# Group-norm statistics averaged on TensorE as a rounded value and its rest, two columns in one single-pass product

## The chip, the core and the metric

The kernel runs on one core of a Trainium2 chip. What counts is device time in microseconds (us) of one execution. The core has five engines with a queue each: TensorE (PE in the profile, with its weight loads listed as PEld), VectorE (DVE), ScalarE (ACT), GpSimd (POOL) and SyncE (SP, which here only starts transfers). Engines wait for one another through semaphores; each runs its own queue in order.

## What is computed

The input is 8 sequences of 512 tokens with 128 features. After a layer norm, four layers of the block below run one after the other, and a mixture of 8 experts is added to the result.

```python
def block(h, p):
    r = _retention(h, wk)                      # masked linear attention
    m = r @ w1 + b1
    a, gate = jnp.split(m, 2, axis=-1)
    m = a * jax.nn.silu(gate) @ w2 + b2
    m = _groupnorm1(m, gg, gb)                 # mean and variance over all tokens AND features
    y = m + h
    f = jax.nn.gelu(y @ wf1 + bf1_, approximate=False) @ wf2 + bf2_
    return (_layernorm(f + y, lg, lb), None)
```

`_groupnorm1` takes one mean and one variance over the 512 x 128 values of a sequence. This document is about how these two numbers are put together.

## The kernel before, in words

Features lie on the 128 partitions, tokens along the free axis, so that the activations of a sequence are one tile of 128 x 512. An item is one sequence in one layer; there are 32, numbered 0 to 31 (item n is sequence n % 8 of layer n // 8). The program of each engine is a loop over slots, `for n in range(ITEMS + ...): slot(n)`, and in each slot every stage handles an item of its own, so that some ten items are in work at once. The order of the stages within a slot is written out by hand for each engine, and the engine follows it in order: an instruction whose semaphore isn't there holds up all that stand behind it.

The eight PSUM banks are shared by stages that take turns. `vacated(n, (reader, back), ...)` makes TensorE wait until the reader of the former contents is through. Bank 4 goes round between projection (`G_BANK`), scores (`SCORE_BANK`), the group-norm averages (`GN_BANK`) and the second half of the feed-forward product (`FEED_B_BANK`).

The group norm of an item goes to and fro between TensorE and VectorE:

- `group_stats`, `group_aggr` (VectorE): mean and variance of each partition, from PSUM. `group_means` adds the bias `B2` to the mean: `gn_m`.
- `group_mean` (TensorE, L388): a product of `mean_of` (128 x 128, all 1/128) with the column `gn_m`; every partition receives the mean over the partitions.
- `group_dev` (VectorE, L897, L898): the deviation `gn_d` of the own mean from it, and `gn_b2`. `group_parts` (L902): `gn_p`, deviation squared plus own variance.
- `group_var` (TensorE, L392): the same kind of product with `gn_p`.
- `group_veps` (VectorE, L907): variance plus epsilon, `gn_v`. It is the last reader of bank 4, and signals `gn_veps`.
- GpSimd's `pow`, then `group_scale`, `group_coef` (VectorE) and `group_norm` (ScalarE).

On VectorE, work for other items stands between these steps: behind `group_means` `set_y` (L929), behind `group_dev` the offsets of another item's layer norm (L956, L959), and between `group_parts` and `group_veps` the steps `gate` (L873), `add_experts` (L981) and `set_z` (L936). On TensorE, `feed_a` (L406) and `feed_b` (L399) stand right behind `group_var`. `feed_b` writes bank 4, so it has this line:

```python
vacated(n, (gn_veps, -1), (gelu_b, 1))
```

that is, it waits for `group_veps` of the item whose averages stand in the bank. The next one behind it, `gram` (L315), waits for `prod_b` of VectorE's `weigh_b` (L967).

A product of float32 operands appears in the trace as two pairs of weight load and multiplication; one of float32r operands (a float32 rounded to what a single pass takes; `xn`, `ot`, `b_w` and `expert_w` are such) as one pair. `product` (L246, L247, L250) makes three single-pass products of rounded values and their rests in place of a float32 one.

Of the kernel before, what the change touches and what calls it, by code (L numbers as in the profile page):

```python
# [5 lines left out]
F32 = mybir.dt.float32  # L6
F32R = mybir.dt.float32r
ALU = mybir.AluOpType
# [3 lines left out]
P = 128  # L12
EPS = 1e-5
# [3 lines left out]
HALF_B1A, HALF_B1G, B1G, B2, GN_G, GN_B, BF1A, BF1B, BF2, LN_G, LN_B = range(11)  # L17
# [8 lines left out]
def retention_moe(nc, x, Wkqv, Wm1, bm1, Wm2, bm2, gn_g, gn_b, Wf1, bf1, Wf2, bf2, ln_g, ln_b,  # L26
# [15 lines left out]
    with ctx:  # L42
        def sb(name, *shape, dtype=F32):
            return ctx.enter_context(nc.sbuf_tensor(name, list(shape), dtype))

        def sem(name):
            return ctx.enter_context(nc.semaphore(name))

        def several(names):
            return [sem(name) for name in names.split()]  # L50
# [6 lines left out]
        mean_of = sb("mean_of", P, P)  # L57
        minus_half = sb("minus_half", P, C)
# [9 lines left out]
        params = sb("params", P, 11, L)  # L68
# [31 lines left out]
        gn_mv = sb("gn_mv", P, 2, 2)  # L100
        gn_m, gn_d, gn_b2, gn_p, gn_v, gn_r, gn_s, gn_c = (
# [35 lines left out]
        GN_BANK = banks[4]  # L137
# [12 lines left out]
        ones_set, means_set, zeros_set, stored = several("ones_set means_set zeros_set stored")  # L150
# [21 lines left out]
        gn_stats, gn_aggr, gn_means, gn_mean, gn_dev, gn_parts, gn_var, gn_veps, gn_rstd, gn_scale, gn_coef, gn_done = several(  # L172
            "gn_stats gn_aggr gn_means gn_mean gn_dev gn_parts gn_var gn_veps gn_rstd gn_scale gn_coef gn_done")
# [55 lines left out]
        def _(pe):  # L229
# [153 lines left out]
            def group_mean(n):  # L383
                if n == 0:
                    pe.wait_ge(means_set, 1)
                pe.wait_ge(gn_means, n + 1)
                vacated(n, (scores_set, -3), (gelu_b, 2))
                pe.matmul(GN_BANK[:, 0:1], mean_of[:, :], gn_m[:, n % 2:n % 2 + 1], start=True, stop=True).then_inc(gn_mean, 1)  # L388

            def group_var(n):  # L390
                pe.wait_ge(gn_parts, n + 1)
                pe.matmul(GN_BANK[:, 2:3], mean_of[:, :], gn_p[:, n % 2:n % 2 + 1], start=True, stop=True).then_inc(gn_var, 1)  # L392
# [333 lines left out]
        def _(dve):  # L726
            def cols(t, n, width=1):
                return t[:, n % 2:n % 2 + 1]
# [160 lines left out]
            def group_means(n):  # L889
                l = n // NB  # L890
                dve.wait_ge(gn_aggr, n + 1)
                dve.tensor_tensor(cols(gn_m, n), gn_mv[:, n % 2, 0:1], params[:, B2, l:l + 1], ALU.add).then_inc(gn_means, 1)

            def group_dev(n):
                l = n // NB
                dve.wait_ge(gn_mean, n + 1)
                dve.tensor_scalar(cols(gn_d, n), GN_BANK[:, 0:1], -1.0, cols(gn_m, n), ALU.mult, ALU.add).then_inc(gn_dev, 1)  # L897
                dve.tensor_scalar(cols(gn_b2, n), GN_BANK[:, 0:1], -1.0, params[:, B2, l:l + 1], ALU.mult, ALU.add)  # L898

            def group_parts(n):  # L900
                dve.wait_ge(gn_dev, n + 1)
                dve.scalar_tensor_tensor(cols(gn_p, n), cols(gn_d, n), cols(gn_d, n), gn_mv[:, n % 2, 1:2],  # L902
                                         ALU.mult, ALU.add).then_inc(gn_parts, 1)

            def group_veps(n):
                dve.wait_ge(gn_var, n + 1)
                dve.tensor_scalar(cols(gn_v, n), GN_BANK[:, 2:3], EPS, None, ALU.add).then_inc(gn_veps, 1)  # L907
# [98 lines left out]
            dve.memset(mean_of[:, :], 1.0 / P).then_inc(means_set, 1)  # L1006
            read_in(0)
# [252 lines left out]
```

## Time and profile before

| | us |
|---|---|
| median of 3 runs | 462.77 (462.64 to 463.01) |
| the profiled execution | 463.61 |
| its span in the profile | 461.7 |
| TensorE busy, share of the span | 440.6, 95% |
| VectorE busy | 385.1, 83% |
| ScalarE busy | 220.0, 48% |
| GpSimd busy | 162.2, 35% |

The span runs from the first to the last instruction; the execution's own time is 1.9 us longer. TensorE's granted clock was 0.992 of full speed over the execution. A busy share says how long an engine had something in it, not that its work set the time; that is read from the chain that ended last, the work that is followed back from the last instruction, at each step to what released it.

### The profile page before, as it was taken

What the parts mean: (1) busy time and instruction counts of PE and PEld (TensorE: products, weight loads), DVE (VectorE), ACT (ScalarE), POOL (GpSimd) and SP (SyncE); (2) the same over time, 40 slices, a digit from 0 to 9 for tenths busy, and PEclk for the clock granted to TensorE, in tenths of its full rate; (3) what the DMA queues carried; (4) which work ended last, traced back from release to release, by engine and by line L of the source; (5) the groups of instructions that cost most, each with busy time, mean ns of one, the idle gap of its engine ahead of it and who ended that gap; (6) DMA issues with size and microseconds to landing.
All of it is one profiled execution on the core that took longest, in us unless ns stands there. A gap on an engine that the chain in (4) does not pass through costs nothing.

```text
span 461.7 us, 7880 instructions
## 1 busy us (share of the span) xinstructions
PE 440.6 (95%) x2302; PEld 318.2 (69%) x2302; DVE 385.1 (83%) x1347; ACT 220.0 (48%) x411; POOL 162.2 (35%) x198
## 2 busy tenths in 40 slices
PE   3999999999999999999999999999999999999982
PEld 2888767777777777777777777777777777765440
DVE  5699989899888877987878877787788887999996
ACT  2125464555554544555555445455555544545331
POOL 3233203634343333542222332433223332334542
PEclk9999999999999999999999999999999999999996
DMA  8900000000000000000000000000000000000113
GB/s 234 253 1 1 1 1 0 2 0 1 1 1 2 1 1 0 2 0 1 1 1 0 2 0 1 1 2 2 1 1 1 1 0 2 1 1 12 34 31 107
DMA packets 13497, 8.20 MB, mean 18 GB/s; under 512 B 608, under 2 KB 13456, under 8 KB 13456
## 3 DMA queue, kind: packets, MB, share of 16 engines
q1 hardware_dynamic: 13376, 7.68, 5.9%
q8 instruction: 20, 0.33, 0.3%
q14 instruction: 21, 0.17, 0.1%
q10 hardware_dynamic: 80, 0.02, 0.0%
HBM read 5.60 MB, written 2.10 MB: 17 GB/s over the span
## 4 chain that ended last, share of the span: by engine, by line
PE 87%; DVE 8%; issue 2%; ACT 1%; DMA 1%; DVEq 0%; POOL 0%; POOLq 0%
PE pair L406 6%; PE bank L325 6%; PE pair L331 6%; PE bank L308 6%; PE bank L381 6%; PE bank L399 6%; PE bank L417 5%; PE bank L254 5%; PE bank L413 5%; PE bank L315 5%; PE bank L250 5%; PE pair L333 4%; PE bank L246 4%; PE bank L247 4%; PE bank L357 3%
## 5 line engine op out<-in xcount | busy, mean ns | idle before, releaser
L1126 POOL TENSOR_TENSOR gn_r<-gn_v,minus_half 128x1 f32<-128x1 f32 x32 | 17.5, 548 | 174.1 <-DVE gn_v L907 174.1
L1136 POOL TENSOR_TENSOR sum_four<-prod 128x512 f32<-128x512 f32 x32 | 40.5, 1265 | 74.6 <-DVE prod L967 74.6
L615 ACT ACTIVATE a_in<-bank,params 128x512 f32<-128x512 f32 x32 | 22.0, 688 | 84.7 <-PE bank L250 84.7
L647 ACT ACTIVATE va<-bank,ln_off,ln_r 128x128 f32<-128x128 f32 x128 | 48.3, 465 | 17.8 <-DVE ln_off L959 17.8
L331 PEld LDWEIGHTS pair<-va,scores 128*128 128x128 f32 x256 | 43.0, 190 | 18.9 <-issue 16.3
L967 DVE TENSOR_TENSOR prod<-bank,route 128x512 f32<-128x512 f32 x64 | 43.7, 683 | 8.6 <-PE bank L250 8.5
L331 PE MATMUL pair<-va,scores 128*128 128x129 f32 x256 | 49.3, 275 | 1.1 <-issue 1.1
L246 PE MATMUL bank<-expert_w,xn 128*128 128x512 f32 x64 | 42.3, 661 | 1.5 <-DVE zt L936 1.5
L325 PEld LDWEIGHTS bank<-gt,vt 128*128 128x128 f32 x256 | 33.5, 191 | 14.5 <-issue 13.1
L1131 POOL TENSOR_TENSOR ln_r<-ln_v,minus_half 128x4 f32<-128x4 f32 x32 | 32.7, 1023 | 14.3 <-DVE ln_v L951 13.5
L333 PE MATMUL pair<-past,gt 128*128 128x129 f32 x192 | 37.1, 275 | 0.0
L315 PEld LDWEIGHTS bank<-va 128*128 128x128 f32 x192 | 27.2, 199 | 14.1 <-issue 14.1
L604 ACT COPY gt<-bank 128x512 f32<-128x512 f32 x32 | 18.7, 585 | 37.0 <-PE bank L308 37.0
L942 DVE BATCH_NORM_STATS2 ln_st<-bank 128x6 f32<-128x128 f32 x128 | 28.4, 283 | 8.8 <-PE bank L254 8.8
L406 PE MATMUL pair<-y,wf 128*128 128x512 f32 x64 | 35.3, 633 | 0.0
L325 PE MATMUL bank<-gt,vt 128*128 128x128 f32 x256 | 33.8, 275 | 0.3 <-ACT gt L604 0.3
L621 ACT ACTIVATE tanh_g<-pair,params 128x512 f32<-128x512 f32 x32 | 22.0, 687 | 25.3 <-PE pair L250 25.3
L381 PE MATMUL bank<-mixed,wm 128*128 128x512 f32 x64 | 33.1, 598 | 0.4 <-ACT gn_out L628 0.4
L308 PE MATMUL bank<-vt,a_w 128*128 128x512 f32 x64 | 33.3, 603 | 0.0
L417 PE MATMUL bank<-gelu,wf 128*128 128x512 f32 x64 | 32.9, 596 | 0.0
L413 PE MATMUL bank<-gelu,wf 128*128 128x512 f32 x64 | 32.9, 595 | 0.0
L399 PE MATMUL bank<-y,wf 128*128 128x512 f32 x64 | 32.8, 594 | 0.0
(159 smaller groups left out, 1097.7 us busy)
## 6 DMA issues: line engine op xcount, KB each, us to landing
x_in<-in_L_attn_x_dram SPq DMA_DIRECT2D x8, 256.0 KB, 5.4
out_dram<-x_in SPq DMA_DIRECT2D x8, 256.0 KB, 2.3
wf<-in_L_attn_Wf_dram SPq DMA_DIRECT2D x2, 512.0 KB, 6.6
kqv<-in_L_attn_Wkqv_dram SPq DMA_DIRECT2D x1, 576.0 KB, 6.2
expert_rows<-in_L_ffn_We_dram SPq DMA_DIRECT2D x1, 512.0 KB, 8.2
wm<-in_L_attn_Wm_dram SPq DMA_DIRECT2D x1, 384.0 KB, 7.2
wm<-in_L_attn_Wm_dram SPq DMA_DIRECT2D x1, 256.0 KB, 5.0
expert_b<-in_L_ffn_be_dram SPq DMA_DIRECT2D x16, 4.0 KB
```

What stands on the lines that cost most here:

```text
L246: pe.matmul(dst, weights(0), moving(0), start=True, stop=False)
L308: pe.matmul(G_BANK[:, :], a_w[:, l, :], vt[:, k, :], start=True, stop=True).then_inc(g_done, 1)
L315: mm = pe.matmul(GRAM_BANK[:, c * AUG:c * AUG + D + 1], va[:, k, c, 0:D], va[:, k, c, 0:D + 1], start=True, stop=True)
L325: mm = pe.matmul(SCORE_BANK[:, of], vt[:, k, of], gt[:, n % 2, of], start=True, stop=True)
L331: mm = pe.matmul(dst, scores[:, n % 2, of], va[:, n % NB, c, 0:D + 1], start=True, stop=(c == 0))
L333: mm = pe.matmul(dst, gt[:, n % 2, of], past[:, n % 3, c - 1, 0:D + 1], start=False, stop=True)
L381: pe.matmul(MIXED_BANK[:, :], wm2[:, n // NB, :], mixed[:, :], start=True, stop=True).then_inc(mixed_done, 1)
L399: pe.matmul(FEED_B_BANK[:, :], wf1[:, n // NB, D:], y[:, n % 2, :], start=True, stop=True).then_inc(f1b_done, 1)
L406: pe.matmul(FEED_A_BANK[:, :], wf1[:, n // NB, 0:D], y[:, n % 2, :], start=True, stop=True).then_inc(f1a_done, 1)
L413: pe.matmul(BACK_BANK[:, :], wf2[:, n // NB, 1, :], gelu[:, n % 2, 1, :], start=True, stop=False)
L417: pe.matmul(BACK_BANK[:, :], wf2[:, n // NB, 0, :], gelu[:, n % 2, 0, :], start=False, stop=True).then_inc(f2_done, 1)
L647: last = act.activation(va[:, n % NB, c, 0:D], Z_BANK[:, c * P:(c + 1) * P], ACT.Identity, bias=ln_off[:, i, c:c + 1], scale=ln_r[:, i, c: ...
```

## The change

Both averages are made as single-pass products in float32r. VectorE writes each of the two inputs as two columns: the value rounded to float32r, and what the rounding left over. One product of the matrix `mean_r` (a float32r copy of `mean_of`) with the two columns gives the averages of both, and the reader adds or subtracts both PSUM columns, as two per-partition scalar operands.

```diff
+        mean_r = sb("mean_r", P, P, dtype=F32R)
+        gn_m2, gn_p2 = (sb(name, P, 2, 2, dtype=F32R) for name in ("gn_m2", "gn_p2"))
...
             def group_mean(n):
                 if n == 0:
-                    pe.wait_ge(means_set, 1)
-                pe.wait_ge(gn_means, n + 1)
+                    pe.wait_ge(mean_r_set, 1)
+                pe.wait_ge(gn_m_rest, n + 1)
                 vacated(n, (scores_set, -3), (gelu_b, 2))
-                pe.matmul(GN_BANK[:, 0:1], mean_of[:, :], gn_m[:, n % 2:n % 2 + 1], start=True, stop=True).then_inc(gn_mean, 1)
+                pe.matmul(GN_BANK[:, 0:2], mean_r[:, :], gn_m2[:, n % 2, :], start=True, stop=True).then_inc(gn_mean, 1)
 
             def group_var(n):
-                pe.wait_ge(gn_parts, n + 1)
-                pe.matmul(GN_BANK[:, 2:3], mean_of[:, :], gn_p[:, n % 2:n % 2 + 1], start=True, stop=True).then_inc(gn_var, 1)
+                pe.wait_ge(gn_p_rest, n + 1)
+                pe.matmul(GN_BANK[:, 2:4], mean_r[:, :], gn_p2[:, n % 2, :], start=True, stop=True).then_inc(gn_var, 1)
...
             def group_means(n):
                 l = n // NB
                 dve.wait_ge(gn_aggr, n + 1)
+                dve.tensor_tensor(gn_m2[:, n % 2, 0:1], gn_mv[:, n % 2, 0:1], params[:, B2, l:l + 1], ALU.add).then_inc(gn_m_rounded, 1)
                 dve.tensor_tensor(cols(gn_m, n), gn_mv[:, n % 2, 0:1], params[:, B2, l:l + 1], ALU.add).then_inc(gn_means, 1)
+                dve.wait_ge(gn_m_rounded, n + 1)
+                dve.wait_ge(gn_means, n + 1)
+                dve.tensor_scalar(gn_m2[:, n % 2, 1:2], gn_m2[:, n % 2, 0:1].bitcast(F32), -1.0, cols(gn_m, n),
+                                  ALU.mult, ALU.add).then_inc(gn_m_rest, 1)
 
             def group_dev(n):
                 l = n // NB
                 dve.wait_ge(gn_mean, n + 1)
-                dve.tensor_scalar(cols(gn_d, n), GN_BANK[:, 0:1], -1.0, cols(gn_m, n), ALU.mult, ALU.add).then_inc(gn_dev, 1)
-                dve.tensor_scalar(cols(gn_b2, n), GN_BANK[:, 0:1], -1.0, params[:, B2, l:l + 1], ALU.mult, ALU.add)
+                dve.tensor_scalar(cols(gn_d, n), cols(gn_m, n), GN_BANK[:, 0:1], GN_BANK[:, 1:2],
+                                  ALU.subtract, ALU.subtract).then_inc(gn_dev, 1)
+                dve.tensor_scalar(cols(gn_b2, n), params[:, B2, l:l + 1], GN_BANK[:, 0:1], GN_BANK[:, 1:2],
+                                  ALU.subtract, ALU.subtract)
 
             def group_parts(n):
                 dve.wait_ge(gn_dev, n + 1)
-                dve.scalar_tensor_tensor(cols(gn_p, n), cols(gn_d, n), cols(gn_d, n), gn_mv[:, n % 2, 1:2],
-                                         ALU.mult, ALU.add).then_inc(gn_parts, 1)
+                dve.tensor_scalar(gn_p2[:, n % 2, 0:1], cols(gn_d, n), cols(gn_d, n), gn_mv[:, n % 2, 1:2],
+                                  ALU.mult, ALU.add).then_inc(gn_p_rounded, 1)
+                dve.tensor_scalar(cols(gn_p, n), cols(gn_d, n), cols(gn_d, n), gn_mv[:, n % 2, 1:2],
+                                  ALU.mult, ALU.add).then_inc(gn_parts, 1)
+                dve.wait_ge(gn_p_rounded, n + 1)
+                dve.wait_ge(gn_parts, n + 1)
+                dve.tensor_scalar(gn_p2[:, n % 2, 1:2], gn_p2[:, n % 2, 0:1].bitcast(F32), -1.0, cols(gn_p, n),
+                                  ALU.mult, ALU.add).then_inc(gn_p_rest, 1)
 
             def group_veps(n):
                 dve.wait_ge(gn_var, n + 1)
-                dve.tensor_scalar(cols(gn_v, n), GN_BANK[:, 2:3], EPS, None, ALU.add).then_inc(gn_veps, 1)
+                dve.tensor_scalar(cols(gn_v, n), GN_BANK[:, 2:3], GN_BANK[:, 3:4], EPS, ALU.add, ALU.add).then_inc(gn_veps, 1)
...
             dve.memset(mean_of[:, :], 1.0 / P).then_inc(means_set, 1)
+            dve.wait_ge(means_set, 1)
+            dve.tensor_copy(mean_r[:, :], mean_of[:, :]).then_inc(mean_r_set, 1)
             read_in(0)
             normalise_in(0)
```

On VectorE four instructions come in for each item. This is its queue around the group norm of one middle item before, from `group_means` (L892) to `group_veps` (L907); a row has line, operation, output, inputs, shape and the semaphores that it waits for:

```order
L892 TENSOR_TENSOR gn_m<-gn_mv,params 128x1 [waits gn_aggr]
L929 SCALAR_TENSOR_TENSOR y<-vt,g_prev,gn_out 128x512 [waits f1b_done,f1a_done,gn_done]
L897 TENSOR_SCALAR gn_d<-bank,gn_m 128x1 [waits gn_mean]
L898 TENSOR_SCALAR gn_b<-bank,params 128x1
L956 TENSOR_TENSOR ln_mr<-ln_mv,ln_r 128x4 [waits ln_rstd]
L959 TENSOR_SCALAR ln_off<-ln_mr 128x4 [waits v_set,ln_mr_set]
L902 SCALAR_TENSOR_TENSOR gn_p<-gn_d,gn_mv 128x1 [waits gn_dev]
L873 SCALAR_TENSOR_TENSOR gated<-pair,params,a_in 128x512 [waits tanh_set,a_in_set]
L981 TENSOR_TENSOR x_in<-x_in,sum_one 128x128 [waits x_shifted,one_set]
L936 SCALAR_TENSOR_TENSOR zt<-bank,params,y 128x512 [waits z_turned,f2_done]
L907 TENSOR_SCALAR gn_v<-bank 128x1 [waits gn_var]
```

And the same place after, as far as `gate`. The names `gn_m` and `gn_p` here stand for both the old tiles and the new `gn_m2` and `gn_p2`:

```order
L894 TENSOR_TENSOR gn_m<-gn_mv,params 128x1 [waits gn_aggr]
L895 TENSOR_TENSOR gn_m<-gn_mv,params 128x1
L898 TENSOR_SCALAR gn_m<-gn_m 128x1 [waits gn_means,gn_m_rounded]
L944 SCALAR_TENSOR_TENSOR y<-vt,g_prev,gn_out 128x512 [waits f1b_done,f1a_done,gn_done]
L904 TENSOR_SCALAR gn_d<-gn_m,bank 128x1 [waits gn_mean]
L906 TENSOR_SCALAR gn_b<-params,bank 128x1
L971 TENSOR_TENSOR ln_mr<-ln_mv,ln_r 128x4 [waits ln_rstd]
L974 TENSOR_SCALAR ln_off<-ln_mr 128x4 [waits v_set,ln_mr_set]
L911 TENSOR_SCALAR gn_p<-gn_d,gn_mv 128x1 [waits gn_dev]
L913 TENSOR_SCALAR gn_p<-gn_d,gn_mv 128x1
L917 TENSOR_SCALAR gn_p<-gn_p 128x1 [waits gn_parts,gn_p_rounded]
L875 SCALAR_TENSOR_TENSOR gated<-pair,params,a_in 128x512 [waits tanh_set,a_in_set]
```

`group_means` has become three instructions (L894, L895, L898) in place of one, the third of which waits for the other two; `group_parts` likewise (L911, L913, L917 in place of L902). Nothing else has moved: `group_veps` (now L922) still stands behind `gate`, `add_experts` and `set_z`.

On TensorE the order of the products is untouched. This is its queue around `group_var` of one middle item before, with `feed_a` and `feed_b` behind it:

```order
L250 MATMUL bank<-expert_w,xn 128x512
L392 MATMUL bank<-gn_p,mean_of 128x1 [waits gn_parts]
L406 MATMUL pair<-y,wf 128x512 [waits o_set,y_set]
L399 MATMUL bank<-y,wf 128x512 [waits gn_veps,y_set]
L315 MATMUL bank<-va 128x129 [waits prod_b,v_set]
```

And after, where line numbers are two higher:

```order
L252 MATMUL bank<-expert_w,xn 128x512
L394 MATMUL bank<-gn_p,mean_r 128x2 [waits gn_p_rest]
L408 MATMUL pair<-y,wf 128x512 [waits o_set,y_set]
L401 MATMUL bank<-y,wf 128x512 [waits gn_veps,y_set]
L317 MATMUL bank<-va 128x129 [waits prod_b,v_set]
```

The product has two columns where it had one, and waits for `gn_p_rest` where it waited for `gn_parts`. `feed_b` still waits for `gn_veps`, and `gram` for `prod_b`.

## Rows read from the trace of the kernel before

**Rows 1.** the page: busy time by engine, and the chain that ended last, by engine
```profile
PE 440.6 (95%) x2302; PEld 318.2 (69%) x2302; DVE 385.1 (83%) x1347; ACT 220.0 (48%) x411; POOL 162.2 (35%) x198
...
PE 87%; DVE 8%; issue 2%; ACT 1%; DMA 1%; DVEq 0%; POOL 0%; POOLq 0%
```

**Rows 2.** chain that ended last: start us, us of the chain, engine, output, line, instructions
```profile
202.99 0.88 PE bank L254 x8
...
210.07 0.11 PE bank L388 x2
210.19 0.50 PE bank L357 x4
...
212.23 0.12 PE bank L392 x2
212.35 0.97 PE pair L406 x2
213.31 0.86 PE bank L399 x2
```

**Rows 3.** timeline of VectorE in the same period: start us, duration us, operation, idle before
```profile
208.69 0.15 DVE L892 TENSOR_TENSOR gn_m<-gn_mv,params 128x1 f32<-128x1 f32 x1
208.75 0.74 DVE L929 SCALAR_TENSOR_TENSOR y<-vt,g_prev,gn_out 128x512 f32<-128x512 f32 x1
210.23 0.22 DVE L897 TENSOR_SCALAR gn_d<-bank,gn_m 128x1 f32<-128x1 f32 x1 [0.73 <-PE bank L388]
...
210.49 0.15 DVE L956 TENSOR_TENSOR ln_mr<-ln_mv,ln_r 128x4 f32<-128x4 f32 x1
210.67 0.17 DVE L959 TENSOR_SCALAR ln_off<-ln_mr 128x4 f32<-128x4 f32 x1
210.75 0.21 DVE L902 SCALAR_TENSOR_TENSOR gn_p<-gn_d,gn_mv 128x1 f32<-128x1 f32 x1
210.90 0.75 DVE L873 SCALAR_TENSOR_TENSOR gated<-pair,params,a_in 128x512 f32<-128x512 f32 x1
...
212.43 0.15 DVE L907 TENSOR_SCALAR gn_v<-bank 128x1 f32<-128x1 f32 x1
```

**Rows 4.** timeline of TensorE in the same period: multiplications, and the weight load (PEld)
```profile
209.91 0.28 PE L388 MATMUL bank<-gn_m,mean_of 128*128 128x1 f32 x2
...
212.72 0.19 PEld L399 LDWEIGHTS bank<-y,wf 128*128 128x128 f32 x1 [0.24 <-issue]
...
213.15 0.59 PE L399 MATMUL bank<-y,wf 128*128 128x512 f32 x1
```

**Rows 5.** timeline of TensorE and VectorE, the same places for item 27
```profile
389.21 0.28 PE L388 MATMUL bank<-gn_m,mean_of 128*128 128x1 f32 x2
...
389.53 0.22 DVE L897 TENSOR_SCALAR gn_d<-bank,gn_m 128x1 f32<-128x1 f32 x1 [0.71 <-PE bank L388]
...
392.10 0.15 DVE L907 TENSOR_SCALAR gn_v<-bank 128x1 f32<-128x1 f32 x1
...
392.36 0.30 PEld L399 LDWEIGHTS bank<-y,wf 128*128 128x128 f32 x2 [0.57 <-issue]
392.45 1.04 PE L399 MATMUL bank<-y,wf 128*128 128x512 f32 x2
```

**Rows 6.** single lines over the whole run: durations ns min/median/max
```profile
L746 DVE TENSOR_SCALAR va<-x_in,in_mv,in_r x32: 332/340/1425, 6.4 to 49.9; 128x128 f32<-128x128 f32 x32
...
L951 DVE TENSOR_SCALAR ln_v<-ln_mv x32: 169/170/922, 77.5 to 450.8; 128x4 f32<-128x4 f32 x32
...
L388 PE MATMUL bank<-gn_m,mean_of x64: 164/250/271, 45.4 to 430.7; 128*128 128x1 f32 x64
```

**Rows 7.** waits over the whole run: us in total, times, longest
```profile
DVE gn_d L897 <- PE bank L388: 17.9, 27, 0.7
```

**Rows 8.** timeline of GpSimd in the period of rows 2
```profile
212.65 0.55 POOL L1126 TENSOR_TENSOR gn_r<-gn_v,minus_half 128x1 f32<-128x1 f32 x1 [4.77 <-DVE gn_v L907]
```

**Rows 9.** one stretch: its length, busy us (instructions) of PE, PEld, DVE, ACT, POOL; clock
```profile
422.00:432.00 10.00, 9.17 (x29) 4.43 (x29) 9.83 (x34) 4.17 (x8) 4.44 (x5) 1.00 0.09 26
```

More of the change, by code:

```diff
@@ L149, in retention_moe @@
         x_loaded = [sem(f"x_loaded{k}") for k in range(NB)]
-        ones_set, means_set, zeros_set, stored = several("ones_set means_set zeros_set stored")
+        ones_set, means_set, mean_r_set, zeros_set, stored = several("ones_set means_set mean_r_set zeros_set stored")
         shift_done, kqv_shifted, kqv_turned, kqv_t_set, folded, a_set, b_rounded, b_set = several(
@@ L171, in retention_moe @@
             "ot_set ot_rest a_in_set tanh_set gated_set mixed_set")
-        gn_stats, gn_aggr, gn_means, gn_mean, gn_dev, gn_parts, gn_var, gn_veps, gn_rstd, gn_scale, gn_coef, gn_done = several(
-            "gn_stats gn_aggr gn_means gn_mean gn_dev gn_parts gn_var gn_veps gn_rstd gn_scale gn_coef gn_done")
+        gn_stats, gn_aggr, gn_m_rounded, gn_means, gn_m_rest, gn_mean, gn_dev, gn_p_rounded, gn_parts, gn_p_rest, gn_var, gn_veps, gn_rstd, gn_scale, gn_coef, gn_done = several(
+            "gn_stats gn_aggr gn_m_rounded gn_means gn_m_rest gn_mean gn_dev gn_p_rounded gn_parts gn_p_rest gn_var gn_veps gn_rstd gn_scale gn_coef gn_done")
         y_set, f1a_done, f1b_done, gelu_a, gelu_b, f2_done, z_set, z_turned = several(
```

## The prediction

> **What bounds the kernel now.** First read the page: TensorE is busy for 95% of the span, and the chain that ended last is 87% TensorE and 8% VectorE [rows 1]. Shorter work on TensorE should shorten the run, if nothing makes TensorE wait in its place. Then the chain itself in one period of the middle, about item 13: TensorE goes from product to product without a gap [rows 2]. VectorE is the follower: between `group_means` and `group_dev` it stands still for 0.73 us until the product of L388 is through [rows 3], and in 27 of the 32 items it waits there [rows 7]. After that, from L897 to L907, it has no idle time at all [rows 3]. That is the stretch to look at, since TensorE's `feed_b` (L399) can't start before `group_veps` (L907) has emptied bank 4.
>
> How much room does that wait have? L907 ends at 212.43 + 0.15 = 212.58. The first weight load of L399 is at 212.72, the multiplication at 213.15 [rows 3, 4]. In item 27, where the VectorE stretch happened to be longer, L907 ends at 392.25 and the load is at 392.36: 0.11 us is the least that the signal takes here. The multiplication follows the load by 0.09 only [rows 5]; I count 0.11, since that is what a load costs where nothing hides it (below). So the room is (0.14 - 0.11) + (0.43 - 0.11) = 0.35 us. Item 27 bears it out: from L897 to the end of L907 it takes 392.25 - 389.53 = 2.72 us, where item 13 takes 212.58 - 210.23 = 2.35, and yet L399 starts 3.24 us after L388 in both (392.45 - 389.21, 213.15 - 209.91) [rows 3, 4, 5]. A delay of 0.37 was just absorbed; little more will be.
>
> **What the change gives TensorE.** A float32 product is two loads and two multiplications. With 1 column to move, the second load lies bare, and so does the first load of the next product. In the chain L388 has 0.11, and the four transposes of L357 behind it take 0.50, where eight elsewhere take 0.88, so 0.06 more than four should: 0.17 in all. L392 has 0.12, and L406 behind it 0.97 where its twin L399 has 0.86: 0.23 in all [rows 2]. The single-pass product keeps one load, which lies under the 512 columns ahead of it as the first one does now. The neighbour's bare load (0.06 and 0.11) stays, with some 0.02 for the short product. Saved: 0.09 + 0.11, so 0.20 us for an item. It can't be over 0.40, the whole of both. The Trainium skill (VectorE: DVE Perf Modes, the section on the TRN2 errata) has a matmul of few columns at 60 cycles, 25 ns at 2.4 GHz: by that the two multiplications that go would give only 0.05. The rows show the bare load as the larger part, and the measurement decides. As L399 turns out below, the sum is the same with either.
>
> **What it costs VectorE**, from start to start. An instruction with no per-partition scalar occupies the queue for 0.06 to 0.07 (L892 to L929), one with one for 0.13 (L897 to L956: two in 0.26). One that needs its predecessor's result starts 0.03 after that has ended (L956 ends at 210.64, L959 starts at 210.67) [rows 3]. Two scalars are seen in L746 alone: 0.34 long, with 128 elements, where L951 without scalars and with 4 elements has 0.17 [rows 6]. If those elements account for about 0.07, each scalar adds 0.05; so I take 0.27 for the duration and 0.185 for the step. Bounds: as with one scalar (0.21 and 0.13), and L746's own 0.34, with a step of 0.26.
>
> - `group_means`: the second `gn_m` starts 0.07 later, the rest waits for its end (0.15 + 0.03), and `set_y` follows 0.13 on: 0.38 in place of 0.07, so +0.31. It is covered by the 0.73 of idle time ahead of `group_dev`. TensorE's product L388 starts at 209.91 [rows 4]; its input is there at 208.84 now and would be at 209.16 after. Without that cover it would cost the 0.31.
> - `group_dev`: two instructions with two scalars, +0.11 (0 to 0.26).
> - `group_parts`: 0.185 to the second, 0.27 + 0.03 until the rest may start, 0.13 to `gate`: 0.62 in place of 0.15, so +0.47 (0.35 to 0.61).
> - `group_veps`: one scalar, ends 0.07 later.
> - `mean_r`: one copy of 128 elements at the start, while VectorE waits for the first input: nothing, at worst L746's 0.34, once.
>
> From L897 to the end of L907 that is +0.65 (0.42 to 0.94). Against it, L897 starts earlier, as one multiplication ends 0.17 after its start where two end after 0.28 [rows 4, 6]: -0.10. Net +0.55 where there is room for 0.35. So L399 starts 3.24 + 0.20 = 3.44 us after L388. Without the wait it would be 3.24 - 0.20 = 3.04, since both savings lie ahead of it. **TensorE then stands still for 0.40 us ahead of `feed_b`**, gives back all it gained, and the period grows by 0.20. Queued behind L399 are `gram` and the next round of everything, so it isn't made up. `prod_b` for `gram` comes late by about as much as L399 itself, and adds nothing. Of the other results that come later on VectorE here (`mixed`, z, the rest of `ot`), the first use stands behind L399 and `gram` in TensorE's queue.
>
> **The sum.** Items 3 to 26 look like item 13: 24 x 0.20 = +4.8 (with the bounds 24 x -0.03 to 24 x +0.49; the upper would need every unknown at its dearest, so I stop halfway at 0.33, +7.9). Item 27 has its room used up by the 0.37 already: +0.5; 28 as the others, +0.2. From item 29 on VectorE has no idle time to hide anything in (9.83 of 10 us [rows 9]), so the full +0.96 of an item (0.31 + 0.11 + 0.47 + 0.07) counts, partly overlapped with TensorE's own work: three items, +2.5. Tail: +3.2 (1.5 to 4.5). Items 0 to 2, where fewer stages run and TensorE waits for this loop: an estimate of +1.0 (0 to 1.5), from up to 0.4 for each plus the late `gate`. Together +9.0. The profiled execution (463.61, 1.9 over its span) would become 472.6; the median of 462.77 stood 0.8 below it, which gives **471.8 us**.
>
> **The rivals.**
>
> - *The late `group_veps`*, as above: 471.8. Chance 0.72.
> - *Two scalars cost no more than one.* Growth 0.42 - 0.10 = 0.32, just under the room of 0.35: L399 starts 0.03 earlier, and only the ends pay. 24 x -0.03 + 1.5 + 0.3 = +1.1, so 463.9. For it: only L746 speaks of two scalars, and its element part is my guess. Chance 0.14, half of it within 0.2%.
> - *TensorE keeps its gain, faster.* One mechanism: `group_veps` comes in time because the new instructions are cheap; from the point where the net growth is under 0.35 there is some gain, and under 0.15 the full one (0.35 less the 0.20 by which TensorE comes early). 27 x -0.20 + 1.0 at the end = -4.4, so 458.4. For it: the 87% of the chain, and a step of 0.07 for plain instructions. Against it: `group_parts` alone has two dependent durations in series, 0.35 at the least by these rows. Chance 0.10.
> - *GpSimd holds up the new instructions.* L951 has a median of 0.17 and a maximum of 0.92 [rows 6], so something stretches small instructions at times. Were it 0.6 more in each of 8 items, that is +4.8, so 476.6. Against it: GpSimd stood idle for 4.77 us up to 212.65 [rows 8], which covers all four new ones. Chance 0.04. The Trainium skill (SBUF — State Buffer, the section on who interferes with whom) makes that lock one between VectorE with two SBUF inputs and GpSimd, for a whole instruction; what rows 8 show leaves it no opportunity in the middle of the run.
>
> Range: the first case from its low side to nearly its high one, and the second: 463.5 to 476. Narrower for the likeliest alone: 467 to 476. About 0.2% (0.9 us) is what a measurement can tell from no change. Faster by more: 0.11 (the third, and a bit of the second). Within: 0.08. Slower: 0.81.
>
> **What would show it.** In the profile after: L399 (now L401) with idle time on TensorE ahead of it of about 0.4 us in each middle period, and its first load 0.11 behind the end of L907 (now L922); L388 as a single multiplication, and the transposes behind it still at 0.50; from the start of `group_dev` to the end of `group_veps` 3.0 us in place of 2.35; `group_parts` spread over 0.62; period 0.20 longer. The prediction is wrong if two-scalar instructions are short, so that this stretch stays under 2.7 us, or if the load of L399 can slip further than 0.32 without its product being late.

## The result, and the profile after

The changed kernel is **slower: 476.98 us** (median of 5 runs, 476.59 to 477.05) against 462.85 (5 runs, 462.64 to 463.59); ratio 1.0281, interval 1.0247 to 1.0315. That is +14.1 us where +9.0 was forecast, and 0.98 us beyond the range's upper end of 476. The profiled execution took 476.70 (span 474.9, which is 13.2 more than the 461.7 of before). Ratios, here and below, are the recorded ones with their 95% intervals, and can differ a little from the quotient of two medians. Some executions in the later sessions, of the kernel before too, had a lower granted clock (down to 0.975) and took up to 6 us longer, so medians below carry 1 to 2 us of scatter and the periods are the sharper measure.

The page of the kernel after, busy time by engine and the chain by engine [for before: rows 1]:
```profile
PE 442.3 (93%) x2238; PEld 308.1 (65%) x2238; DVE 413.3 (87%) x1476; ACT 221.4 (47%) x411; POOL 162.2 (34%) x198
...
PE 60%; DVE 28%; issue 10%; DMA 1%; DVEq 1%; ACT 0%; POOL 0%; POOLq 0%
```
64 multiplications and 64 loads are gone, and 129 VectorE instructions have come, with 28 us of busy time. TensorE's busy time has not shrunk: part of a wait is booked as busy there, as shown below. The plainest sign is the chain of work that ended last. TensorE's share fell from 87% to 60%, and VectorE's rose from 8% to 28%.

A period is the time from one item's mean product to the next one's. One period of that chain, about item 13 (start us, us of the chain, engine, output, line) [rows 2]:
```profile
214.79 0.05 PE bank L390
214.84 0.03 issue
214.87 0.04 DVE gn_d L904
...
217.07 0.74 DVE zt L951
217.81 0.14 DVE gn_v L922
217.95 0.14 issue
218.09 1.10 PE bank L401 x2
219.18 0.67 PE bank L317 x6
...
227.83 0.05 PE bank L390
```
Before, the chain never left TensorE in this stretch. Now it goes out to VectorE at L390 and comes back at L401 (`feed_b`, L399 before). From the mean product to the end of `feed_b` it takes 219.18 - 214.79 = 4.39 us, where it took 213.31 + 0.86 - 210.07 = 4.10: +0.29, and this period is 227.83 - 214.79 = 13.04.

VectorE in the same period (start us, duration us, operation, idle time before it) [rows 3]:
```profile
214.87 0.28 DVE L904 TENSOR_SCALAR gn_d<-gn_m,bank 128x1 f32<-128x1 f32 x1 [0.24 <-PE bank L390]
215.07 0.27 DVE L906 TENSOR_SCALAR gn_b<-params,bank 128x1 f32<-128x1 f32 x1
...
215.52 0.27 DVE L911 TENSOR_SCALAR gn_p<-gn_d,gn_mv 128x1 fp32r<-128x1 f32 x1
215.71 0.26 DVE L913 TENSOR_SCALAR gn_p<-gn_d,gn_mv 128x1 f32<-128x1 f32 x1
216.08 0.21 DVE L917 TENSOR_SCALAR gn_p<-gn_p 128x1 fp32r<-128x1 f32 x1
216.21 0.74 DVE L875 SCALAR_TENSOR_TENSOR gated<-pair,params,a_in 128x512 f32<-128x512 f32 x1
...
217.07 0.74 DVE L951 SCALAR_TENSOR_TENSOR zt<-bank,params,y 128x512 f32<-128x512 f32 x1
217.73 0.21 DVE L922 TENSOR_SCALAR gn_v<-bank 128x1 f32<-128x1 f32 x1
```
The idle time ahead of `group_dev` shrank from 0.73 to 0.24, since `group_means` takes more and the shorter product is through earlier (`group_dev` starts 0.24 after it, and 0.32 before); from there to the end of `group_veps` VectorE needs 217.94 - 214.87 = 3.07 us where it needed 2.35. Look at L917: L913 has ended at 215.97, and L917 starts only at 216.08, 0.11 later.

TensorE and its weight loads (PEld) in the same period, GpSimd's row, and the mean product of items 3 and 27 [rows 4, 5, 8]:
```profile
83.59 0.17 PE L390 MATMUL bank<-gn_m,mean_r 128*128 128x2 f32 x1
...
214.63 0.17 PE L390 MATMUL bank<-gn_m,mean_r 128*128 128x2 f32 x1
...
216.68 0.17 PE L394 MATMUL bank<-gn_p,mean_r 128*128 128x2 f32 x1
216.71 1.10 PE L408 MATMUL pair<-y,wf 128*128 128x512 f32 x2
218.02 0.55 POOL L1143 TENSOR_TENSOR gn_r<-gn_v,minus_half 128x1 f32<-128x1 f32 x1 [5.39 <-DVE gn_v L922]
218.06 0.30 PEld L401 LDWEIGHTS bank<-y,wf 128*128 128x128 f32 x2 [1.07 <-issue]
218.09 1.10 PE L401 MATMUL bank<-y,wf 128*128 128x512 f32 x2 [0.27 <-DVE gn_v L922]
...
398.48 0.17 PE L390 MATMUL bank<-gn_m,mean_r 128*128 128x2 f32 x1
```
L401's load is at 218.06, 0.12 behind the end of `group_veps` at 217.94. The multiplication is recorded 0.03 after its load, yet it has 1.10 us in the chain, against 0.86 in [rows 2]: these 0.24 are the rest of the wait, booked as work. That is why the page's busy time for TensorE went up.

The waits over the whole run, total us, times and longest [rows 7]:
```profile
DVE gn_d L904 <- PE bank L390: 5.5, 22, 0.3
```
And the view of single lines over the whole run: durations of L390 and L917, ns min/median/max [rows 6], and under L922 who waited for it, us and times:
```profile
L390 PE MATMUL bank<-gn_m,mean_r x32: 164/165/272, 45.3 to 443.2; 128*128 128x2 f32 x32
...
L917 DVE TENSOR_SCALAR gn_p<-gn_p x32: 212/214/217, 46.6 to 445.5; 128x1 fp32r<-128x1 f32 x32
...
L922 DVE TENSOR_SCALAR gn_v<-bank x32: 209/211/217, 47.7 to 446.5; 128x1 f32<-128x1 f32 x32
...
  PE bank L401: 9.0, 28
```
L390 is one multiplication of 165 ns where L388 was two. In 28 of 32 items TensorE has recorded idle time ahead of `feed_b`. Between 90 and 350 us the kernel before has no wait of TensorE for VectorE at all.

A stretch near the end: its length, busy us of PE, PEld, DVE, ACT and POOL, then the granted clock [rows 9]:
```profile
435.00:445.00 10.00, 8.28 (x24) 3.72 (x24) 9.72 (x32) 2.99 (x6) 4.42 (x5) 1.00 0.09 28
```
VectorE is busy for 9.72 of 10 us and TensorE for 8.28, and the chain runs through VectorE there, as before. The granted clock is 1.00 in this stretch, falls to 0.50, the lower of its two levels, only for the last 7.5 us of the span (7.6 before), and is 0.992 over the whole of either execution; it has no part in the loss.

Where the 13.2 us of the span lie, by the start of the mean product in items 3 and 27 (the periods of the middle are 13.04 to 13.14 long, 13.07 in the mean, but for items 10, 17 and 19; those of before are 12.76, but for items 3 and 19):

| stretch | before | after | difference | forecast |
|---|---|---|---|---|
| up to item 3 | 82.05 | 83.59 | +1.5 | +1.0 |
| item 3 to 27, 24 periods | 307.16 | 314.89 | +7.7 | +4.8 |
| item 27 to the end of the span | 72.5 | 76.4 | +3.9 | +3.2 |

### The profile page after: what moved, and what is told of

The parts are those of the page before. It is cut to its first block, busy times and chain, and to the rows that moved or that the text cites. A ratio compares the mean times of both kernels' runs of the same rounds, so it can differ in the third digit from the quotient of the medians.

```text
span 474.9 us, 7945 instructions
## 1 busy us (share of the span) xinstructions
PE 442.3 (93%) x2238; PEld 308.1 (65%) x2238; DVE 413.3 (87%) x1476; ACT 221.4 (47%) x411; POOL 162.2 (34%) x198
## 4 chain that ended last, share of the span: by engine, by line
PE 60%; DVE 28%; issue 10%; DMA 1%; DVEq 1%; ACT 0%; POOL 0%; POOLq 0%
PE bank L401 6%; PE pair L333 6%; PE bank L310 5%; PE bank L327 5%; PE bank L256 5%; PE bank L383 5%; PE bank L317 5%; DVE zt L951 4%; PE bank L415 4%; PE pair L335 4%; PE bank L248 3%; PE bank L252 2%; PE bank L249 2%; DVE prod L982 2%; DVE gn_b L906 2%
## 5 line engine op out<-in xcount | busy, mean ns | idle before, releaser
L401 PE MATMUL bank<-y,wf 128*128 128x512 f32 x64 | 34.9, 627 | 9.1 <-DVE gn_v L922 9.0
L317 PEld LDWEIGHTS bank<-va 128*128 128x128 f32 x192 | 27.1, 199 | 14.2 <-issue 14.2
```

What stands on the lines that cost most here:

```text
L317: mm = pe.matmul(GRAM_BANK[:, c * AUG:c * AUG + D + 1], va[:, k, c, 0:D], va[:, k, c, 0:D + 1], start=True, stop=True)
L401: pe.matmul(FEED_B_BANK[:, :], wf1[:, n // NB, D:], y[:, n % 2, :], start=True, stop=True).then_inc(f1b_done, 1)
```

## The experiments

**Theory A**, as in the prediction: `feed_b` is gated by the path `group_dev` to `group_veps` on VectorE, with room for 0.35 us. While this path grows by less, TensorE keeps at least a part of its gain; over it, the gain and the excess are lost. **Rivals**: the costs simply add (each new instruction costs its time, whatever TensorE does), and VectorE as a whole has become too full, at 87%.

### One half of the change at a time

The mean alone in the new form (`group_var`, `group_parts` and `group_veps` as before):
```diff
-pe.matmul(GN_BANK[:, 2:4], mean_r[:, :], gn_p2[:, n % 2, :], start=True, stop=True).then_inc(gn_var, 1)
+pe.matmul(GN_BANK[:, 2:3], mean_of[:, :], gn_p[:, n % 2:n % 2 + 1], start=True, stop=True).then_inc(gn_var, 1)
...
```


> Only the mean is averaged the new way; the variance keeps its float32 product, its one instruction and its one column. Theory A: from the start of group_dev to the end of group_veps only the two subtractions grow (+0.13), against 0.08 of earlier start: within the room of 0.35. So L388's half of TensorE's gain stays (0.11 x 24 = 2.6), and the ends lose about 2 for the 0.44 more on VectorE: 462.2. Theory B: 0.44 of 1.12 us of new VectorE work, so 40% of the 14.1 lost: 468.5.

Measured: 463.78 us (10 runs), ratio 0.999 (0.9953 to 1.0027), span 460.1, period 12.65. TensorE doesn't wait between items 3 and 27, and the period is 0.11 shorter than the 12.76 of before. The extra instructions of `group_means` and `group_dev` are paid outside the middle: the 24 periods give 2.5 back, and from item 27 on 1.2 are lost again. The way from item 0 to item 3 takes 0.5 more too (37.19 against 36.67), though item 0 starts 0.8 earlier in this execution and hides it.

The variance alone (`group_mean`, `group_means` and `group_dev` as before):
```diff
-pe.matmul(GN_BANK[:, 0:2], mean_r[:, :], gn_m2[:, n % 2, :], start=True, stop=True).then_inc(gn_mean, 1)
+pe.matmul(GN_BANK[:, 0:1], mean_of[:, :], gn_m[:, n % 2:n % 2 + 1], start=True, stop=True).then_inc(gn_mean, 1)
...
```


> Only the variance is averaged the new way; the mean keeps its float32 product and its old instructions. Theory A: the path grows by 0.54 in group_parts and 0.07 in group_veps, 0.61 against 0.35 of room: TensorE waits ahead of L401, and the period is 12.76 + 0.26 = 13.02, 24 x 0.26 + 3 at the ends: 472. The gain on L392 is lost whole. Theory B: 60% of 14.1: 471.3. It is the middle period and the idle time ahead of L401 that tell, not the total.

Measured: 473.53 us (4 runs), ratio 1.0193 (1.013 to 1.0257), period 13.00 to 13.03, 13.01 in the mean. The load of `feed_b` comes 0.12 behind the end of `group_veps` in every item of the middle. The halves are -0.11 and +0.25 for a period, but both together are +0.30: behind the wait that the variance half opens, the mean half no longer gives its 0.11, and costs 0.05, by its longer `group_dev`. The wait itself comes from `group_parts`, with 0.06 more from the longer `group_veps`.

### The new VectorE work with the old products

```diff
-pe.matmul(GN_BANK[:, 0:2], mean_r[:, :], gn_m2[:, n % 2, :], start=True, stop=True).then_inc(gn_mean, 1)
+pe.matmul(GN_BANK[:, 0:1], mean_of[:, :], gn_m[:, n % 2:n % 2 + 1], start=True, stop=True).then_inc(gn_mean, 1)
...
-pe.matmul(GN_BANK[:, 2:4], mean_r[:, :], gn_p2[:, n % 2, :], start=True, stop=True).then_inc(gn_var, 1)
+pe.matmul(GN_BANK[:, 2:3], mean_of[:, :], gn_p[:, n % 2:n % 2 + 1], start=True, stop=True).then_inc(gn_var, 1)
```
`group_dev` and `group_veps` are those of before; the rounded parts and rests are made, but TensorE multiplies the float32 values.

> The new VectorE instructions of group_means and group_parts are all there, and TensorE waits for the rests, but both averages are the float32 products of before, and group_dev and group_veps read one column as before; the rounded columns are computed and not used. So it has VectorE's cost without TensorE's gain. Theory A: TensorE's gain never counted in the middle, since it lies ahead of the wait in L401. L401 comes at 0.32 + 2.35 + 0.54 + 0.12 + 0.11 = 3.44 us after the product of the mean, period 12.96; with ends of +4.5 that is 462.85 + 24 x 0.20 + 4.5 = 472. Rival C, the sum: cost and gain add, the changed kernel is 14.1 slower in spite of 0.22 gained for each item, so without the gain this one (whose path is shorter by the 0.20 of group_dev and group_veps) is at 477 + 32 x 0.22 - 24 x 0.20 = 479.

Measured: 473.2 us (4 runs), ratio 1.021 (1.0193 to 1.0227). The chain that ended last, the mean product of two items:
```profile
202.40 0.11 PE bank L390 x2
...
215.36 0.12 PE bank L390 x2
```
The period is 12.96 (12.93 to 12.97, 12.95 in the mean). If costs and gains added, taking the gain of 0.22 away from the changed kernel, and the 0.19 by which `group_dev` and `group_veps` are shorter here (2.88 from start to end, for 3.07), would make 13.07 + 0.22 - 0.19 = 13.10. It is 12.95: the gate gives it, as 0.19 are taken from the path and `group_dev` starts 0.08 later. But for these 0.08, TensorE's saving is worth nothing in the changed kernel, as forecast: it only comes earlier to the same wait.

### The new products without their price

This kernel leaves out the rests: the second column of each product is a constant, so the statistics are those of the rounded values only.
```diff
-dve.tensor_tensor(gn_m2[:, n % 2, 0:1], gn_mv[:, n % 2, 0:1], params[:, B2, l:l + 1], ALU.add).then_inc(gn_m_rounded, 1)
-dve.tensor_tensor(cols(gn_m, n), gn_mv[:, n % 2, 0:1], params[:, B2, l:l + 1], ALU.add).then_inc(gn_means, 1)
+dve.tensor_tensor(gn_m2[:, n % 2, 0:1], gn_mv[:, n % 2, 0:1], params[:, B2, l:l + 1], ALU.add).then_inc(gn_means, 1)
...
+dve.tensor_copy(gn_m2[:, :, 1], mean_of[:, 0:2])
```


> Leaves out part of the computation: only the rounded value is averaged, no rest is computed; the second column is a constant that nobody reads, so that the two products of TensorE are exactly those of the changed kernel. VectorE has as many instructions as before. It measures TensorE's gain alone. Theory A: no wait ahead of L401, 0.22 less for each item (0.11 at either product), period 12.54, 462.85 - 30 x 0.22 = 456.3. If the gain were only that of two short multiplications (0.05), it would be 461.3.

Measured: 457.52 us (10 runs), ratio 0.9899 (0.9869 to 0.9929), span 455.7. The chain that ended last:
```profile
207.52 0.00 PE bank L390
...
220.09 0.00 PE bank L390
```
The 0.11 of L388 [rows 2] has become 0.00, and the period is 12.57, so 0.19 to 0.20 shorter. `feed_b` starts 3.02 after the mean product where it was 3.24: the two products together save 0.22 up to there (0.20 forecast), of which the period keeps 0.20. The Trainium skill (VectorE: DVE Perf Modes, the section on the TRN2 errata) has a matmul of few columns at 60 cycles, from which, as an estimate, 0.05 would follow for the two multiplications that go. This run shows over four times that for the two products; that rule is for the multiplication alone, and here a weight load goes with each.

### The wait for two semaphores

Before each rest the changed kernel waits for the semaphore of the rounded part and for that of the float32 value. Here both producers raise one semaphore, and there is one wait:
```diff
-                                  ALU.mult, ALU.add).then_inc(gn_p_rounded, 1)
+                                  ALU.mult, ALU.add).then_inc(gn_parts, 1)
...
-dve.wait_ge(gn_p_rounded, n + 1)
-dve.wait_ge(gn_parts, n + 1)
+dve.wait_ge(gn_parts, 2 * n + 2)
```


> The changed kernel, but both instructions ahead of each rest signal the same semaphore, so that the rest waits for one count instead of two semaphores. Theory: the gap ahead of the rest is 0.10 to 0.11 us with two waits and 0.03 with one, as at L971 to L974. In group_parts it lies on the path to group_veps, so every middle period gets 0.07 shorter: 24 x 0.07 + 0.5 at the ends, 477.0 - 2.2 = 474.8. Rival: the gap belongs to the instruction and not to the number of waits, no change, 477.0.

Measured: 473.65 us (4 runs), ratio 1.0235 (1.0198 to 1.0272), period 13.00. Timeline of VectorE in item 13:
```profile
213.47 0.27 DVE L910 TENSOR_SCALAR gn_p<-gn_d,gn_mv 128x1 fp32r<-128x1 f32 x1
213.65 0.27 DVE L912 TENSOR_SCALAR gn_p<-gn_d,gn_mv 128x1 f32<-128x1 f32 x1
213.95 0.22 DVE L915 TENSOR_SCALAR gn_p<-gn_p 128x1 fp32r<-128x1 f32 x1
214.08 0.74 DVE L875 SCALAR_TENSOR_TENSOR gated<-pair,params,a_in 128x512 f32<-128x512 f32 x1
```
The rest now starts 0.03 after L912 ends (213.92), not 0.11, and `group_parts` spreads over 214.08 - 213.47 = 0.61, which is the 0.62 of the prediction. The mean period falls by 0.07 (13.07 to 13.00), as expected. Items 3 to 27 take 312.53 where they took 314.89: 24 x 0.07 = 1.7, and 0.7 because two pauses of VectorE that the changed kernel has (last section) don't lie on its path here. With 1.0 up to item 3 and 0.6 from item 27 on, it is 4.0 us of span, more than the 2.2 expected.

The kernels in the order of before can be set side by side. Each column but the last is read from item 13 of its trace; "sum" adds 0.11 for the load, and what it exceeds 3.24 by should be the growth of the period. The last column is the mean over items 4 to 26, without 10 and 17 to 19:

| kernel | `group_dev` starts after the mean product | to the end of `group_veps` | to the load | sum | over 3.24 | period over 12.76 |
|---|---|---|---|---|---|---|
| after | 0.24 | 3.07 | 0.12 | 3.54 | +0.30 | +0.30 |
| one semaphore | 0.24 | 3.01 | 0.12 | 3.48 | +0.24 | +0.23 |
| variance only | 0.32 | 2.95 | 0.12 | 3.50 | +0.26 | +0.25 |
| vector work only | 0.32 | 2.88 | 0.12 | 3.43 | +0.19 | +0.19 |
| mean only | 0.23 | 2.46 | 0.12 | 2.92 | none | -0.11 |

### Is there a second gate behind the first?

If `group_veps` is late, let it run ahead of `set_z`, which nobody on TensorE needs so soon:
```diff
                 step(add_experts, n - 12)
-                step(set_z, n - 10)
                 step(group_veps, n - 8)
+                step(set_z, n - 10)
                 step(weigh_b, n - 10)
```


> The changed kernel with group_veps moved ahead of set_z in VectorE's slot (two adjacent stages swapped), nothing else. Theory A, the gate: the loss in the middle comes from group_veps alone, which empties bank 4 too late for feed_b. set_z takes 0.66 us in the queue, so group_veps ends 0.66 earlier, with its room back. TensorE has no idle time ahead of L401 and the middle period is 12.76 - 0.20 = 12.56 us; the ends, where VectorE has no idle time, keep their loss (about 1.5 at the start, 3.9 at the end): 462.85 - 24 x 0.20 + 5.4 = 463.5 us. Theory B, the load: VectorE has 1.1 us more to do for each item and is too full wherever that stands: the period stays near 13.05 and the time at 475 to 477.

Measured: 469.45 us (10 runs), ratio 1.0102 (1.0066 to 1.0138), period 12.80 where 12.56 was expected. The wait at `feed_b` is gone, and half of the gain doesn't come. Timeline of TensorE, its loads and VectorE in item 14 of this kernel:
```profile
227.74 0.22 DVE L922 TENSOR_SCALAR gn_v<-bank 128x1 f32<-128x1 f32 x1
228.32 1.02 PE L401 MATMUL bank<-y,wf 128*128 128x512 f32 x2
228.53 0.68 DVE L982 TENSOR_TENSOR prod<-bank,route 128x512 f32<-128x512 f32 x1
229.33 0.74 PEld L317 LDWEIGHTS bank<-va 128*128 128x128 f32 x6 [0.81 <-issue]
229.36 0.91 PE L317 MATMUL bank<-va 128*128 128x129 f32 x6
```
TensorE's part of its chain, one item earlier:
```profile
215.70 0.86 PE bank L401 x2
216.56 0.91 PE bank L317 x6
```
`feed_b` comes early and is as short as it was before. But now the products of `gram` (L317) have 0.91 in the chain instead of 0.67: their first load is at 229.33, 0.12 behind the end of `prod_b` at 228.53 + 0.68 = 229.21. `weigh_b`, which makes `prod_b`, still stands behind `set_z`. In the changed kernel this second gate is hidden behind the first: there L317's load goes at 218.65, 0.53 ahead of its multiplications at 219.18 in the chain. Remove the first gate, and the second takes 0.24 of every period.

The same swap with the kernel before:


> The kernel before with the same swap of group_veps and set_z. Control for the run above. Theory A: group_veps had 0.35 us of room already and more of it is worth nothing: 462.8, period 12.76. Theory B says the same. If the time falls by more than 0.5 us, the swap brings a gain of its own, which must be taken off the run above.

Measured: 466.22 us (10 runs), ratio 1.0036 (0.9999 to 1.0073), period 12.82. A period of 12.76 and 462.8 were expected. Here VectorE reaches `group_veps` before the product of L392 is through and stands still for 0.54 us in nearly every item, with `set_z` and `prod_b` queued behind it; `gram`'s load goes at 4.02 after the mean product instead of 3.67, and the chain has the 0.06 of the period in `gram` and the products right behind it. Another 0.75 lies between items 3 and 4 (13.74 for 12.99).

So both stages have to run ahead of `set_z` (with one semaphore as above):
```diff
-                step(set_z, n - 10)
                 step(group_veps, n - 8)
                 step(weigh_b, n - 10)
+                step(set_z, n - 10)
```


> The changed kernel with one semaphore for each pair, and group_veps and weigh_b both moved ahead of set_z, in all 32 items. The run with group_veps alone ahead showed no wait in L401 any more, but one in gram (L317), whose weight load came 0.12 us after the end of weigh_b: a second gate right behind the first. Theory A2, two gates in a row: with both results early the middle period is 12.76 - 0.20 = 12.56, the ends still lose 4 to 5: 462.8 - 24 x 0.20 + 4.5 = 462.5. Theory B, VectorE too full: period 12.75 or more, 467 or more.

Measured: 464.47 us (12 runs), ratio 1.0021 (0.9988 to 1.0054), span 461.2. Timeline of VectorE and TensorE in item 13:
```profile
211.24 0.22 DVE L920 TENSOR_SCALAR gn_v<-bank 128x1 f32<-128x1 f32 x1
211.37 0.68 DVE L980 TENSOR_TENSOR prod<-bank,route 128x512 f32<-128x512 f32 x1
...
211.90 1.02 PE L401 MATMUL bank<-y,wf 128*128 128x512 f32 x2
212.75 0.83 PE L317 MATMUL bank<-va 128*128 128x129 f32 x6
```
`prod_b` is there at 212.05, 0.70 ahead of `gram`, and the mean products of the chain stand at 209.04 and 221.60: period 12.56 to 12.57, the same as in the kernel with the rests left out. All new VectorE instructions are in this kernel, and VectorE is busy for 89% of its span. So VectorE isn't too full; two results stood at the wrong places in its order. What is lost now lies outside the middle: 0.6 between items 3 and 4 (13.62 for 12.99), and from item 27 on it needs 75.8 us against 72.5. That takes back what the middle gains; 462.5 was expected.

### What the new form is worth where it is hidden

`split(n)` is `2 <= n < 28`: only these items use the new form, since VectorE has no idle time at the end to hide anything. First with `group_veps` alone ahead of `set_z`:
```diff
+                if split(n):
+                    mm = pe.matmul(GN_BANK[:, 0:2], mean_r[:, :], gn_m2[:, n % 2, :], start=True, stop=True)
+                else:
+                    mm = pe.matmul(GN_BANK[:, 0:1], mean_of[:, :], gn_m[:, n % 2:n % 2 + 1], start=True, stop=True)
+                mm.then_inc(gn_mean, 1)
```


> Group_veps ahead of set_z, one semaphore for each pair, and the new form only for items 2 to 27, where TensorE is the bound; items 0, 1 and 28 to 31 use the float32 products and the old instructions. Theory A: period 12.54 in the middle, little lost at the ends: 462.85 - 24 x 0.22 + 0.5 = 458.1, faster than both kernels. Theory B: VectorE too full in the middle: 470 or more.

Measured: 465.22 us (10 runs), ratio 1.0041 (1.0005 to 1.0077), period 12.74. The expectation of 458.1 missed by 7 us, and the period of this kernel says where most of it lies, 24 x 0.2 = 4.8: `gram` has 0.85 in its chain, where 0.67 is the value without a wait. It is the second gate again, and confining the new form to the middle doesn't touch it. In the profiled execution a further 3 us lie ahead of item 3 (85.13 for 82.05), where the granted clock is 0.50 for 3.4 us twice, from 22.3 and from 53.1.

The same with both stages ahead of `set_z`:


> The same order of group_veps, weigh_b and set_z, but the new form only for items 2 to 27; items 0, 1 and 28 to 31 use the float32 products and the old instructions. Theory A2: period 12.56 in the middle and almost nothing lost at the ends: 462.8 - 25 x 0.20 + 0.3 = 458.1, faster than both kernels. Theory B: 463 or more.

Measured: **461.15 us** (12 runs), ratio 0.9959 (0.9921 to 0.9996), span 459.1, period 12.57. It beats both kernels, by 0.4% against the one before, though its interval reaches almost to 1, and 458.1 was expected. The new order is in it too, and has to be told apart by the kernel before in that same order:


> Control: the kernel before with group_veps and weigh_b ahead of set_z. There neither result was waited for, so earlier ones bring nothing; but VectorE now stands still for the product L392, as it did with group_veps alone ahead (0.54 us in each period). Period 12.76, 462.8, at most 0.5 more at the ends. If it is faster, the order alone has a gain, and the run above must be held against this one.

Measured: 465.8 us (12 runs), ratio 1.0039 (1.0016 to 1.0063), span 464.0, period 12.76. The order alone changes nothing in the middle and costs 2.2 us of span outside it, where at most 0.5 was expected: 0.8 between items 3 and 4 and 1.4 behind item 27. This is its chain near the end:
```profile
448.28 0.68 DVE prod L967
448.96 0.67 DVE zt L936
449.63 0.04 issue
449.67 0.50 PE bank L246
...
451.07 2.01 PE bank L436 x2
```
The experts' products of the last items (L246) wait for z, and z now stands behind `prod_b`. That makes 1.0 of the 1.4: L246 starts 59.6 us after item 27's mean product, and 58.6 before. The rest shows with the clock. TensorE stood idle for 1.85 us ahead of this L246 (1.31 before), and from 451.0 on its granted clock is 0.50, where the kernel before keeps 1.00 up to 454.1; L436 takes 2.07 us instead of 1.12, and VectorE waits 0.33 for it. Against this control the new form in the middle saves 465.8 - 461.15 = 4.65 us, which is 24 x 0.19 to 0.20 = 4.6 to 4.8 by the periods: all of TensorE's gain. An order that changes only in the middle would be near 461.15 - 2.2 = 459 us; this is an estimate, and it wasn't tried.

Last, the part that never needed another order, the mean alone in items 2 to 27, in the order of before:


> Old order of the stages, and only the mean averaged the new way (with one semaphore), in items 2 to 27; everything else as before. The run with the mean alone in all items had a period of 12.65 and lost time at the ends. Theory A: 12.65 kept, the ends as before: 462.8 - 25 x 0.11 + 0.2 = 460.2, with nothing moved.

Measured: 461.88 us (12 runs), ratio 0.997 (0.994 to 1.0001), span 459.6, period 12.65. The 24 periods give back 2.6 us, the first items cost 0.4, and the end 0.1. The median is 1.7 above the 460.2 expected; the period is the one expected.

## Why the prediction was right, and where its sizes were off

- **Direction and mechanism: right.** The chain, the wait at L401 and the load 0.12 behind `group_veps` are there as forecast, and the table ties the period of the four gated kernels to that one path within 0.01 us. Only sizes were off: the loss was 14.1 us instead of 9.0, beyond the range, whose upper end stopped halfway to the dearest sum.
- **What the change gives TensorE: right.** 0.22 against 0.20 (the kernel with the rests left out). All of it but an earlier start of `group_dev` is lost in the changed kernel, as the kernel with the new VectorE work and the old products shows.
- **Two scalars: right.** 0.27 in L911 as assumed. The rival in which two scalars cost no more than one falls; so does the one in which TensorE keeps its gain.
- **`group_parts`: the term that was mis-sized.** The prediction let the rest start 0.03 after its predecessor's end. It is 0.11 in the changed kernel, so 0.69 instead of 0.62, and 0.61 where both producers raise one semaphore. The step had been taken from L956 and L959 [rows 3]. L959 waits for two semaphores too, but only one of them is raised by an instruction right ahead of it, so it was no example of this case. The same gap makes `group_means` 0.40 longer instead of 0.31; the idle time behind it covered that.
- **`group_dev`**: its start came 0.24 after the mean product instead of 0.22, and this with the gap makes 3.53 to 3.54 for `feed_b` where 3.44 was forecast. The period grew by 0.29 to 0.30 instead of 0.20; 24 x 0.09 = 2.2 of the missing 4.2 us of span.
- **"Idle time on TensorE ahead of it of about 0.4"**: the record shows 0.27, and 0.24 more are inside L401's own 1.10. The two together, 0.51, are the wait. Whoever reads only the recorded idle time would have found the prediction too high where it was too low.
- **The 24 periods** hold a further 0.7, about 0.33 in each of items 10 and 17 (last section). No term of the prediction has these.
- **Item 27 ("room used up by the 0.37 already: +0.5")**: wrong. The longer stretch there was a pause of VectorE of this same kind (below). It lies elsewhere in the changed kernel, and item 27's period is 13.04, +0.28 over before.
- **Items 0 to 2**: +1.5, the upper end of the estimate of 0 to 1.5. **Tail**: +3.9 inside its bounds of 1.5 to 4.5. Together 1.2 of the missing 4.2.
- **"`prod_b` for `gram` comes late by about as much as L399 itself, and adds nothing"**: right for the changed kernel (`prod_b` is 0.65 later, `feed_b` ends 0.29 later, and `gram` doesn't wait), and misleading for anyone who would repair it. It was the second gate, close behind the first and worth 0.24 for an item.
- **GpSimd holding up the new instructions: no.** L917 has 212 to 217 ns in all 32 items, and of the other new ones a single L894 is longer, 356 ns for a median of 148.

## What to carry to other kernels

When a follower engine has idle time, ask in which place: time ahead of a wait hides what is added ahead of that wait, and nothing behind it. When work between a late result and its reader grows, list all readers in order with the slack of each, since the next gate shows only once the first is gone; here two results had to move ahead of one 0.7 us stage that nobody needed yet. And use a trade of engines only in those items in which the receiving engine has the room: the same new form cost 14 us everywhere and in the old order, and was 4.65 us ahead of its control in the middle and in a better one.

## What the runs showed of the hardware that was not expected

- A small VectorE instruction that needs the results of the two instructions right ahead of it starts 0.11 us after the last of them has ended when each raises a semaphore of its own (L913 to L917), and 0.03 after when both raise one. Two waits alone don't make the gap: L959 waits for two semaphores as well, `ln_mr_set` of L956 and `v_set`, and starts 0.03 after L956 has ended [rows 3]. There the wait for the instruction right ahead comes first in the program, and in L917 it comes second. Whether that order matters, or that both semaphores are VectorE's own and fresh, wasn't tried.
- With one element for each partition, VectorE takes 0.15 us without a per-partition scalar, 0.21 or 0.22 with one and 0.27 or 0.28 with two, and the next independent instruction starts 0.07, 0.13 and 0.19 to 0.20 after it.
- A float32 product of one column has 0.11 us in the chain, and the single-pass product of two columns has 0.00, though the weight load that goes is recorded with 0.19. And a multiplication that waits for its load can be recorded 0.03 after the load's start, so that part of a wait counts as busy time.
- In two items of the changed kernel VectorE stood still where it should not have. Timeline of VectorE in item 17:
```profile
267.96 0.26 DVE L913 TENSOR_SCALAR gn_p<-gn_d,gn_mv 128x1 f32<-128x1 f32 x1
268.68 0.21 DVE L917 TENSOR_SCALAR gn_p<-gn_p 128x1 fp32r<-128x1 f32 x1 [0.46 <-DVE gn_p L913]
```
  L917 starts 0.46 after L913 has ended, 0.35 more than in the other items; in item 10 there are 0.24 of idle time ahead of `gate`. This is no accident of one execution: the kernel with `group_veps` ahead and the one with the new VectorE work and the old products pause at the very same two places, by 0.24 and 0.46, and each of the two kernels with one half of the change by 0.24 in item 18. The kernel before has it in item 27, and it is what made that stretch longer in [rows 5]:
```profile
390.57 0.75 DVE L873 SCALAR_TENSOR_TENSOR gated<-pair,params,a_in 128x512 f32<-128x512 f32 x1 [0.30 <-issue]
```
  The kernel with one semaphore has 0.25 ahead of L942 at 212.06, just before item 13's mean product, where VectorE would wait for TensorE anyway, so it costs nothing. The place thus moves with the program. Ten of the fourteen traces have a pause of this kind, and behind each of them an 8 KB transfer on an instruction queue (q14) starts within 0.6 to 1.0 us (at 391.2 in the kernel before, at 177.6 and 269.4 in the changed one); many such transfers have no pause ahead of them. That the fetching of instructions causes the pauses is a guess; no run tried it.
